# Three dense layers moved ahead of the transposes, and the transposes among the table lookups moved later, in a recommendation tower

## The reference

```python
e = jnp.stack([tbl_0[ids[:, 0]], ..., tbl_31[ids[:, 31]]], axis=1)   # 512 x 32 x 256
z = jnp.einsum('bnd,bmd->bnm', e, e)[:, iu, ju]                      # the pairs i < j: 512 x 496
h = jnp.concatenate([z, dense_ctx], axis=1)                          # 512 x 512
h = jnp.maximum(h @ W_top1 + b_top1, 0.0)                            # 512 x 512
h = jnp.maximum(h @ W_top2 + b_top2, 0.0)                            # 512 x 256
y = h @ W_top3                                                       # 512 x 1
```

## Time and profile before

| | us |
|---|---|
| time, median of 3 runs | 160.71 (160.5 to 161.36) |
| time of the profiled execution | 161.99 |
| its span, first to last instruction | 160.0 |
| TensorE busy in the span | 144.8 (90%) |
| GpSimd (POOL) busy in the span | 104.8 (66%) |

### The profile page before, as it was taken

One profiled execution on the slowest core, in us unless ns is written; L12 is line 12 of the kernel. 1 busy time (PEld: TensorE's weight loads), 2 busy tenths in 40 slices (PEclk: granted clock), 3 DMA queues, 4 the chain that ended last, 5 costly groups with the idle time before them and its releaser, 6 DMA issues.

```text
span 160.0 us, 4655 instructions
## 1 busy us (share of the span) xinstructions
PE 144.8 (90%) x1878; PEld 125.1 (78%) x1878; DVE 90.3 (56%) x288; ACT 73.4 (46%) x179; POOL 104.8 (66%) x110
## 2 busy tenths in 40 slices
PE   6999999898999997899778979899799697999994
PEld 6788888686868886798667969599699496997883
DVE  3899986747557014999625844618536341653500
ACT  3357887572864616475431435323253502452411
POOL 1578777878777777777777777777777777710000
PEclk9999999999999999999999999999999999999998
DMA  4999999787557567533333333333334333320000
GB/s 126 257 328 361 370 279 283 190 221 221 166 166 222 160 234 246 178 113 106 102 114 109 115 99 110 111 113 110 98 102 120 115 108 102 100 73 1 6 4 1
DMA packets 11519, 24.15 MB, mean 151 GB/s; under 512 B 3062, under 2 KB 3538, under 8 KB 11499
## 3 DMA queue, kind: packets, MB, share of 16 engines
q0 software_dynamic: 4992, 13.64, 29.4%
q1 hardware_dynamic: 6362, 9.97, 19.9%
q10 hardware_dynamic: 144, 0.26, 0.6%
HBM read 23.74 MB, written 0.00 MB: 148 GB/s over the span
## 4 chain that ended last, share of the span: by engine, by line
PE 55%; POOL 20%; DMA 14%; issue 9%; DVE 1%; SPq 0%; ACT 0%; POOLq 0%
POOL rows L394 20%; PE bank L613 18%; DMA rows<-table,row_ids 13%; PE bank L663 12%; PE xt_ps L633 9%; PE bank L669 6%; PE xt_ps L767 2%; PE bank L733 2%; PE xt_ps L740 2%; PE bank L705 2%; DMA pairs<-pairs 1%; PE bank L747 1%; SPq L350 0%; PE xt_ps L747 0%; DVE pairs L441 0%
## 5 line engine op out<-in xcount | busy, mean ns | idle before, releaser
L394 POOL DMA_INDIRECT rows<-table,row_ids x104 | 104.1, 1001 | 35.1 <-issue 26.5
L512 ACT COPY xt<-xt_ps 128x512 f32<-128x512 f32 (+1 forms) x45 | 23.3, 549 | 48.5 <-PE xt_ps L633 48.3
L633 PE MATMUL xt_ps<-ident,rows 128*128 128x128 f32 x208 | 31.7, 281 | 10.0 <-DMA rows<-table,row_ids 9.4
L633 PEld LDWEIGHTS xt_ps<-ident,rows 128*128 128x128 f32 x208 | 22.5, 140 | 16.7 <-DMA rows<-table,row_ids 7.5
L663 PE MATMUL bank<-xt 128*64 128x64 f32 x1024 | 33.7, 224 | 1.1 <-ACT xt L521 1.0
L663 PEld LDWEIGHTS bank<-xt 128*64 128x64 f32 x1024 | 31.4, 138 | 3.6 <-ACT kept L507 1.2
L445 DVE COPY pairs<-bank 32x48 f32<-32x48 f32 x138 | 27.8, 202 | 2.2
L413 DVE TENSOR_SCALAR one_hot<-small_ids_sb,first_sb 128x512 fp32r<-128x512 int32 x48 | 22.3, 499 | 10.5 <-PE bank L613 10.4
L613 PE MATMUL bank<-one_hot,high 128*128 128x512 f32 x96 | 26.4, 396 | 0.0
L613 PE MATMUL bank<-one_hot,low 128*128 128x512 f32 x96 | 25.9, 391 | 0.0
L424 DVE COPY xt<-xt_ps 128x512 f32<-128x512 f32 (+1 forms) x14 | 8.3, 596 | 29.7 <-PE xt_ps L633 29.6
(11 more groups left out here) (39 smaller groups left out, 55.7 us busy)
## 6 DMA issues: line engine op xcount, KB each, us to landing
small_sb<-small_tables SPq DMA_DIRECT2D x23, 256.0 KB, 5.1
rows<-table,row_ids POOLq DMA_INDIRECT x104, 2.8
w_sb<-w SPq DMA_DIRECT2D x6, 256.0 KB, 3.5
small_ids_sb<-small_ids SPq DMA_DIRECT2D x5, 256.0 KB, 6.3
w_sb<-w SPq DMA_DIRECT2D x1, 512.0 KB
small_ids_sb<-small_ids ACTq DMA_DIRECT2D x1, 256.0 KB, 3.8
small_sb<-small_tables SPq DMA_DIRECT2D x2, 128.0 KB, 3.6
ids_sb<-ids SPq DMA_DIRECT2D x1, 100.0 KB, 3.4
```

The costliest lines, as they stand in the source:

```text
L394: nc.gpsimd.indirect_dma_start(rows[:, i % ROWS, :], None, table, bass.IndirectOffsetOnAxis(ap=row_ids[:, i:i + 1], axis=0)).then_inc(gath ...
L512: nc.scalar.copy(*fill_parts(f)).then_inc(xt_act, 1)
L633: last = nc.tensor.transpose(to, rows[:, i % ROWS, c * P:(c + 1) * P], ident[:])
```

## The change

Five things are done:

1. Fills among the lookups stand one or two pairs of chunks later, and fills 18 and 19 leave them for round 0: `EARLY` is 18 in place of 20. Fill 18 goes from ScalarE to VectorE with it.
2. The layers move. Layer 1 of a block is still begun behind the fills of rounds 4, 8 and 12 (three of eight halves), but the other five halves stand between the dot products and the fills of the next round. Layer 2 of a block moves from behind the fills of rounds 7 and 11 to ahead of the fills of rounds 6 and 10, and layer 3 from behind the fills of rounds 8 and 12 to ahead of those of rounds 7 and 11. ScalarE's activations move along.
3. The first batch's last looked-up field goes from its bank straight to `xt`: one copy of 128x32 by ScalarE and one by VectorE. The other five fields are copied from `kept` before.
4. ScalarE takes the last lookup bank to `kept` only after the fills behind pair 23.
5. One of POOL's waits (`PAUSED_FOR_PRODUCTS`) is gone.

```diff
-FILLS_BEHIND = {6: (0, 1, 2), 9: (3, 4, 5), 11: (6, 7, 8), 14: (9, 10, 11), 17: (12, 13, 14), 20: (15, 16, 17),
-                23: (18, 19)}
-EARLY = 20
-PAUSED_FOR_LOOKUPS, PAUSED_FOR_PRODUCTS = 15, 18
+FILLS_BEHIND = {6: (0, 1, 2), 9: (3, 4, 5), 13: (6, 7, 8), 16: (9, 10, 11), 19: (12, 13, 14), 22: (15, 16), 23: (17,)}
+EARLY = 18
+PAUSED_FOR_LOOKUPS = 15
...
-FILLS_IN = [1, 2, 1, 2, 2, 3, 2, 3, 3, 2, 3, 2, 3, 4, 6]
+FILLS_IN = [3, 2, 1, 2, 2, 3, 2, 3, 3, 2, 3, 2, 3, 4, 6]
...
-RELU1_IN = {7: 0, 11: 1, 14: 2}
+LAYER1_IN = {5: (0, [3, 4, 5, 6, 7]), 9: (1, [3, 4, 5, 6, 7]), 13: (2, [3, 4, 5, 6, 7])}
+LAYER1_BEHIND = {4: (0, [0, 1, 2]), 8: (1, [0, 1, 2]), 12: (2, [0, 1, 2])}
+RELU1_IN = {5: 0, 9: 1, 13: 2}
+LAYER2_IN = {6: 0, 10: 1}
+LAYER3_IN = {7: 0, 11: 1}
...
+        def first_batch_parts():
+
+            return xt[:, 0, :, :, GATHERED:N_FIELDS - 1], kept[:, :, 0:SAMPLES, 0:LOOKED_UP - 1]
+
+        def first_batch_found(c):
+
+            return xt[:, 0, c, :, N_FIELDS - 1], banks[FOUND_BANKS[LOOKED_UP - 1][c]][:, 0:SAMPLES]
...
-                    if e >= PAUSED_FOR_PRODUCTS:
-
-                        pool.wait_ge(dots_half_done, 1)
...
             dve.wait_ge(chunk_used, LOOKED_UP * CHUNKS)
+            nc.vector.tensor_copy(*first_batch_found(DC - 1)).then_inc(first_batch_dve, 1)
...
-                keep_found(two)
+                if two < TWOS - 1:
+                    keep_found(two)
+                if 2 * (two + 1) == (LOOKED_UP - 1) * CHUNKS:
+
+                    act.wait_ge(found_kept, kept_of(LOOKED_UP - 1))
+                    nc.scalar.copy(*first_batch_parts())
                 if two == TWOS - 1:
-                    take_kept(0)
+                    act.wait_ge(chunk_used, LOOKED_UP * CHUNKS)
+                    nc.scalar.copy(*first_batch_found(0)).then_inc(kept_act, 1)
                 for f in FILLS_BEHIND.get(two, ()):
                     take_xt(f)
+                if two == TWOS - 1:
+                    keep_found(two)
...
                     pe.wait_ge(found_kept, kept_of(PRODUCTS_FREE))
+                    pe.wait_ge(first_batch_dve, 1)
...
                 dots(2 * r + 1)
+                if r in LAYER2_IN:
+                    layer2_of(LAYER2_IN[r])
+                if r in LAYER3_IN:
+                    layer3(LAYER3_IN[r], l3_ps)
+                if r in LAYER1_IN:
+                    b, halves = LAYER1_IN[r]
+                    for i in halves:
+                        layer1_half(b, i)
...
-                if r in LAYER2_BEHIND:
-                    layer2_of(LAYER2_BEHIND[r])
-                if r in LAYER3_BEHIND:
-                    layer3(LAYER3_BEHIND[r], l3_ps)
+                if r == ROUNDS - 1:
+                    layer3(NB - 2, l3_ps)
```

More of the change, by code:

```diff
@@ L68 @@
            10: (15,)}
-FILLS_IN = [1, 2, 1, 2, 2, 3, 2, 3, 3, 2, 3, 2, 3, 4, 6]
+FILLS_IN = [3, 2, 1, 2, 2, 3, 2, 3, 3, 2, 3, 2, 3, 4, 6]
 ROUNDS = len(FILLS_IN)
-LAYER1_BEHIND = {4: (0, [0, 1, 2]), 5: (0, [3, 4, 5]), 6: (0, [6, 7]), 8: (1, [0, 1, 2]), 9: (1, [3, 4, 5]),
-                 10: (1, [6, 7]), 12: (2, [0, 1, 2, 3, 4]), 13: (2, [5, 6, 7])}
-RELU1_IN = {7: 0, 11: 1, 14: 2}
-LAYER2_BEHIND = {7: 0, 11: 1}
-RELU2_IN = {8: 0, 12: 1}
-LAYER3_BEHIND = {8: 0, 12: 1, 14: 2}
-Y_IN = {9: 0, 13: 1}
+LAYER1_IN = {5: (0, [3, 4, 5, 6, 7]), 9: (1, [3, 4, 5, 6, 7]), 13: (2, [3, 4, 5, 6, 7])}
[3 more added lines that the diff above has]
+LAYER3_IN = {7: 0, 11: 1}
 FOUND_BANKS = [(2, 3), (0, 1)] * 3
@@ L175, in build_tower @@
         last_kept_dve = sem("last_kept_dve")
+        first_batch_dve = sem("first_batch_dve")
         gathered = [sem(f"gathered{n}") for n in range(ROWS)]
@@ L574, in _ @@
                     take_kept(n)
-                if r in RELU2_IN:
-                    relu2(RELU2_IN[r], l2_ps, range(N2))
-                if r in Y_IN:
-                    keep_y(Y_IN[r], l3_ps)
+                if r in LAYER2_IN:
+                    relu2(LAYER2_IN[r], l2_ps, range(N2))
+                if r in LAYER3_IN:
+                    keep_y(LAYER3_IN[r], l3_ps)
                 if r in RELU1_IN:
```

## The result

The changed kernel takes 160.37 us (median of 20 runs, 158.56 to 162.17), the kernel before on the same chips 161.63 us (20 runs, 160.50 to 162.86). The ratio is 0.9906, interval 0.988 to 0.9932, and the quotient of the two medians 0.9922: the changed kernel is 0.8 to 0.9% faster. The forecast of 159.4 stood on a base of 160.71, a ratio of 0.9918, inside that interval; the base itself measured 0.9 us higher once more runs were made. Executions of one kernel spread over 2% and more here, and the ratios of this document leave out those more than 1.5% above the fastest (five of the changed kernel's 20, none before), so a ratio and the quotient of two medians can differ by half a per cent.

The account below looks back on a forecast made before the run. POOL's gathers were taken as a fixed clock, so only PE work between gather 97 and the last fills counts. Six steps from 126.25 put dots 14 at 136.55, not 137.83: 1.28 us off the 160.71 median, 159.4; range 158.1 to 160.8.

Parts of the forecast that it names:

- What bounds the kernel: POOL's 104 gathers, 1.25 us each, never wait; only PE work between gather 97 and 143.29 us counts.
- The lookups: Edits ahead of the rounds: rounds start 2 to 4.5 us sooner, worth nothing at the end.
- Rounds 8 to 12: Same PE work reordered, 20.04 us plus 0.6: PE ready for gather 90 at 123.2, 3.0 us before it lands.
- Steps 1 to 4: PE from gather 90 at 126.25: transposes, 18 layer-1 records, dots 13, 30 layer-1 records, to 134.31.
- step 1: Gather 90's two transposes on PE: 0.33 us, to 126.58.
- step 3: Dot products of batch 13 on PE: 2.08 us, to 130.77.
- step 4: 30 layer-1 records on PE: 3.54 us, to 134.31.
- Steps 5 and 6: Fills 49 to 52, with the relu ahead of ScalarE's copies, to 136.48; dots 14 start at 136.55, 1.28 us gained.
- The clock of gathers: VectorE's subtractions stretch gathers they meet; about as many meetings after the change, so nothing, bounds 0.9 us each way.
- the gain drowns in the copies: Rival: ScalarE's queue behind the relu runs 0.6 us or more later, half the gain gone, 160.4; chance 0.2.
- The clock of gathers runs ahead: Rival: 2.5 of the gathers' 5.3 us extra go, everything from gather 90 sooner, 156.9; chance 0.07.
- PE's clock falls: Rival: idling PE falls to 1.2 GHz; behind gather 90 one group costs 1.8 us (161.2), behind gather 71 covered; chance 0.08.

Follow-up runs that it names:

- e1: The changed kernel with the dense layers put back where they stood before; ratio to the kernel before 1.0044.
- e10: The changed kernel with the first three halves of block 1's layer 1 between the first two fills of round 8; ratio to the kernel before 0.9935.
- e6: The changed kernel with VectorE's subtractions of low shortened to 8 columns and high multiplied twice, leaving the low part out; 156.86 us, ratio 0.9722.
- e5: The changed kernel with the relu of block 2's layer 1 behind ScalarE's copies of round 13; ratio to the kernel before 0.9937.
- e3: The kernel before with only block 2's remaining layer 1 (five halves, with its relu) moved ahead of round 13's fills; ratio 0.9955.
- e4: The changed kernel with block 2's layer 1 and its relu put back where they were; ratio to the kernel before 0.9996.
- e2: The kernel before with the layers alone moved as in the change; ratio 0.9941.
- e7: The changed kernel with block 2's layer 1 begun one round sooner, ahead of round 12's fills; ratio to the kernel before 0.9893.
- e9: The changed kernel with each subtraction of low cut into four pieces of 128 columns, same result; ratio to the kernel before 0.9946.
- e11: The changed kernel with round 14's layer 2 of block 2 behind the first three last fills, batch 15's first dot products behind the last; ratio 0.9906.

## Why the prediction was right

- **What bounds the kernel** (the gathers as a clock, read between gather 97 and the last fills): shown. e1 moves the rounds 4.2 us and the end not at all; e10 moves PE 1.1 us and the tail not at all; e6 moves the gathers 4.25 us and the end 3.91.
- **The lookups**, worth nothing at the end: shown by e1. I forecast batch 0's dot products 2 to 4 us sooner; they came 4.0 sooner.
- **Rounds 8 to 12**: dot products of batch 12 end at 122.96 (forecast 123.2), still ahead of gather 90.
- **Steps 1 to 4**: gather 90's transposes at 126.50 where I started the sum at 126.25; with that the 30 records end at 134.35 (forecast 134.31), because the four steps took 134.35 − 126.50 = 7.85 us where their terms add up to 8.06 (step 1 took 0.28 for 0.33, step 3 2.01 for 2.08, step 4 3.45 for 3.54).
- **Steps 5 and 6**: 136.66 for 136.55. The total holds, its reading does not: e5 shows that the relu in front of the copies is covered by PE's own transposes. What stands on the path is 14 transposes and the copy of fill 52 behind them, for which PE waits 0.54 us.
- **Gain**: 143.29 − 142.12 = 1.17 us at the last fills (forecast 1.28), 1.3 us in the span (158.7, as forecast). The exact hit is partly luck: behind the gathers the change gained more, 1.59 us of tail and 1.46 us at batch 14's dot products against the last gather, and gathers that ended 0.29 us later took the difference back. e3 and e4 show that block 2's layer 1 is the part without which there is none, and that by itself it gives half.
- **The median**: 160.37 for 159.4, inside the range (158.1 to 160.8). The forecast stood on a median of three runs before, and this one moved from 160.71 to 161.63; the difference of the medians, 1.26 us, is the 1.3 forecast.
- **The clock of gathers**: taken as unchanged with 0.9 us either way; it moved 0.29. That the subtractions stretch the gathers was argued from one pair of rows; e6 shows it.
- **Rival "the gain drowns in the copies"**: fell; ScalarE's wait is 0.54 us, and e5 takes nothing off it. **"The clock of gathers runs ahead"**: did not happen here, but e6 forces it and lands at 156.86. **"PE's clock falls"**: not in the profiled execution of the changed kernel, but real in those of e2, e4, e5, e6, e7 and e9 (0.50 to 0.75 granted over 4 us between 98 and 106), at the first of the two places that I named. I had its chance as that of the whole result; it is an event of single executions: 9 of the 20 runs of the changed kernel had a mean clock under 0.985, and 11 of the 93 runs of the kernel before that were made beside the experiments. Its price behind gather 71 is some 0.5 us (e5; 0.6 in e2), where I had written that it is covered: the slack left out ten transposes. Over the 20 runs, the median span of those nine is 158.5 us and of the other eleven 158.1.

## What to carry to other kernels

When one engine issues at a fixed pace and never waits, as POOL does here, the busiest engine is not the bound until the last thing that it waits for: look for that place, and count only the work behind it. Work moved from behind it to ahead of it gains the idle time that it fills, less the wait that it lays bare, and not its own length: the 18 records moved in e3 take 2.11 us and gave 0.74 at batch 14's dot products, for a wait of 1.05 us filled and one of 0.54 opened. Work removed ahead of it gained nothing (e1, e10). To compare two executions, measure the distance from the pacing engine's last instruction to the end, since the pace itself differs from one execution to the next.

## What the runs showed that I had not expected

- Subtractions cut in four hold a gather as long as the whole does (e9: it ends 0.92 us behind the last piece).
- Executions of one kernel spread over 3.6 us with the long subtractions and 0.21 us with short ones (e6, four executions).
- A packet of instructions meets every sixth to eighth gather, which then lands late; in e2 and e5 that was gather 90, on which the end depends, and PE waited 0.7 and 0.9 us for it.
- The clock fell to 1.2 GHz behind the sparse waits of round 8 with PE busy 2.33 us of 4, (e5), and held with 2.36 (the changed kernel) and with 1.65 (e11). The Trainium skill, TensorE: Matmul & The Clock Gate, Part 1, has an idle engine fall to 1.2 GHz and recover when it works again; the runs agree that it falls after waits and recovers, and show that short transposes between the waits do not always prevent it. Whether a given execution falls stays open.
